# High and low position rows interleaved: four position transfers a phase in place of eight

## What is computed

```
x = x + L0(group_norm(x))     # 12 heads of 16 channels, all 1024 keys, softmax
x = x + L1(group_norm(x))     # the same heads, keys within a 7 by 7 window, and 16 register keys
```

```
rel_h = einsum('bhwc,hkc->bhwk', q, Rh)      # one value for each query and key row
rel_w = einsum('bhwc,wkc->bhwk', q, Rw)      # one value for each query and key column
scores = q @ k.T * 16**-0.5 + rel_h[..., :, None] + rel_w[..., None, :]
```

## Time and profile before

| What | Value |
|---|---|
| median of three executions | 6088.66 us (6077.25 to 6094.65) |
| the profiled execution | 6093.63 us, its span 6091.8 us |
| TensorE (PE) busy | 4712.5 us, 77% |
| VectorE (DVE), ScalarE (ACT), GpSimd (POOL) busy | 51%, 43%, 15% |
| mean granted clock of TensorE | 0.861 of full |
| DMA on SP's queue | 184672 packets, 266.11 MB, 15.5% of 16 engines' span |

### The profile page before, as it was taken

One profiled execution on the slowest core, in us unless ns is written; L12 is line 12 of the kernel. 1 busy time (PEld: TensorE's weight loads), 2 busy tenths in 40 slices (PEclk: granted clock), 3 DMA queues, 4 the chain that ended last, 5 costly groups with the idle time before them and its releaser, 6 DMA issues.

```text
span 6091.8 us, 97943 instructions
## 1 busy us (share of the span) xinstructions
PE 4712.5 (77%) x32598; PEld 2332.9 (38%) x32598; DVE 3078.8 (51%) x5558; ACT 2622.6 (43%) x3955; POOL 892.4 (15%) x1899
## 2 busy tenths in 40 slices
PE   3768877788777878777878777787778877778788
PEld 2233443444424444343433434434344443434334
DVE  2536555455554545544545454555545455545553
ACT  1333434344453444434445354444534445344454
POOL 3111100111101111011111111111011110111100
PEclk6777888888888988888889888888889889888898
DMA  5223221322213322123221223222133221332211
GB/s 102 61 59 74 49 70 55 80 64 63 56 49 80 71 62 65 39 75 76 70 62 46 72 63 77 64 58 64 50 80 69 63 65 36 80 76 70 57 35 32
DMA packets 231273, 386.23 MB, mean 63 GB/s; under 512 B 53788, under 2 KB 129120, under 8 KB 230752
## 3 DMA queue, kind: packets, MB, share of 16 engines
q1 hardware_dynamic: 184672, 266.11, 15.5%
q10 hardware_dynamic: 21504, 75.51, 6.3%
q0 software_dynamic: 24576, 37.80, 3.8%
HBM read 227.79 MB, written 88.08 MB: 52 GB/s over the span
## 4 chain that ended last, share of the span: by engine, by line
PE 40%; DMA 27%; SPq 23%; DVE 5%; issue 4%; ACT 2%; DVEq 0%; POOL 0%; ACTq 0%
DMA AR<-biases 15%; SPq L488 15%; PE P L1123 8%; PE P L1141 7%; PE P L1085 7%; DMA biases<-xn 6%; PE P L948 4%; PE P L949 4%; SPq L500 4%; DMA queries<-oraw 3%; DMA A<-mrow 3%; DVE mx L891 2%; SPq L475 2%; SPq L467 2%; PE P L1173 2%
## 5 line engine op out<-in xcount | busy, mean ns | idle before, releaser
L891 DVE TENSOR_REDUCE mx<-P 128x1 f32<-128x512 f32 x3072 | 1906.3, 682 | 1375.5 <-PE P L1085 1367.7
L761 ACT ACTIVATE probs<-P 128x1024 f32<-128x1024 f32 x1536 | 1505.4, 1022 | 1298.4 <-PE P L1141 1296.0
L1085 PE MATMUL P<-K,AR 96*128 96x256 f16 x6144 | 1163.0, 299 | 618.5 <-DMA AR<-biases 592.9
L777 ACT ACTIVATE probs<-P 128x320 f32<-128x320 f32 (+3 forms) x1632 | 638.9, 436 | 887.8 <-PE P L1194 545.5
L1085 PEld LDWEIGHTS P<-K,AR 96*128 96x128 f16 x6144 | 552.1, 104 | 1211.6 <-issue 398.9
L1141 PE MATMUL P<-AR,K 113*128 113x512 f16 x3072 | 951.2, 394 | 2.2 <-DVE mx L891 1.2
L1123 PE MATMUL P<-probs,V 128*17 128x512 f32 x6144 | 860.7, 634 | 9.9 <-ACT probs L761 9.9
L897 DVE TENSOR_REDUCE mxc<-P 128x1 f32<-128x336 f32 (+1 forms) x1536 | 646.5, 475 | 368.7 <-PE P L1094 368.4
L1061 PE MATMUL P<-QA,Z 128*128 128x64 f16 x3072 | 267.9, 253 | 302.9 <-DMA biases<-xn 225.4
L1141 PEld LDWEIGHTS P<-AR,K 113*128 113x128 f16 x3072 | 223.4, 99 | 716.8 <-ACT probs L761 528.9
L1194 PE MATMUL P<-A,K 113*128 113x320 f16 (+2 forms) x1536 | 467.5, 316 | 13.7 <-ACT probs L777 12.7
(11 more groups left out here) (120 smaller groups left out, 3740.5 us busy)
## 6 DMA issues: line engine op xcount, KB each, us to landing
AR<-biases SPq DMA_DIRECT2D x768, 128.0 KB
AR<-queries ACTq DMA_DIRECT2D x96, 512.0 KB
biases<-xn SPq DMA_DIRECT2D x192, 256.0 KB, 7.2
AR<-queries ACTq DMA_DIRECT2D x96, 256.0 KB
K<-oraw POOLq DMA_DIRECT2D x384, 64.0 KB, 4.7
xin<-in_x_dram SPq DMA_DIRECT2D x16, 768.0 KB, 9.4
queries<-oraw SPq DMA_DIRECT2D x384, 32.0 KB, 5.0
QA<-queries SPq DMA_DIRECT2D x192, 64.0 KB, 3.5
```

Of the source, the lines that this page charges most:

```text
L761: nc.scalar.activation(probs[:, u % RING, j:j + 2, :], P[:, b:b + 2, :], ACT.Exp).then_inc(p_done[0], 1)
L777: nc.scalar.activation(probs[:, full % RING, j, 0:n], P[:, step % SCORES[1], 0:n], ACT.Exp).then_inc(p_done[1], 1)
L891: V_.reduce_max(mx[:, n // 2, n % 2:n % 2 + 1], bank, AX.X).then_inc(used, 1)
L1085: last = mm(bank[:, QD * (v % 2):QD * (v % 2) + QD], AR[0:ROWS_MAX[0], part % SLOTS, v, c, j, 128 * q:128 * q + 128], K0[0:ROWS_MAX[0], h, ...
```

## The change

`biases` is laid out with the key index outermost and the high or low part behind it, so that high and low rows of one key lie side by side. The rows of `AR` and the patterns of `K0` take the same order: row 2k is the high and row 2k + 1 the low part of key k. The source of a fill is then 32 evenly spaced rows of 4 KB. A fill is four DMAs, one for each table and block of 16 keys, each of which writes the two equal variants from one source that is read twice (256 KB written a DMA). `biases_away` writes rows that are 16 KB apart. The count on `ar_in` goes from ten to six DMAs a phase.

```diff
@@ -236,7 +236,7 @@
         K0 = sb("K0", [128, NH, S], F16)
         A1, K1 = sb("A1", [128, NH, S], F16), sb("K1", [128, NH, KW], F16)
         queries = nc.dram_tensor("queries", (G, 2, D, 4, GH, QD), F16).ap()
-        biases = nc.dram_tensor("biases", (G, 2, 2, 32, 4, GH, QD), F16).ap()
+        biases = nc.dram_tensor("biases", (G, 2, 32, 2, 4, GH, QD), F16).ap()
         mid = nc.dram_tensor("mid", (B, 128, TT, C), F32).ap()
         V = [sb(f"V{n}", [128, TT, NH, D + 1]) for n in range(2)]
         vreg = sb("vreg", [128, G, 128])
@@ -333,7 +333,7 @@
         res_done = sems("res_done")
         out_in = sem("out_in")
         PER_ITEMS = [PHASES[n] * (ITEMS[n] + 1) for n in range(2)]
-        PER_Q, PER_K, PER_QA, PER_AR = 12 * 16, 12 * 16, 4 * 16, 10 * 16
+        PER_Q, PER_K, PER_QA, PER_AR = 12 * 16, 12 * 16, 4 * 16, 6 * 16
         PER_QUERIES, PER_BIASES = (8 * 16, 16 * 16), 4 * 16
         PER_MROW = (VAR * 16, 16)
         SUM_STEPS, POOL_STEPS = 3 * TT - 2, 3 * TT - 2 + 5
@@ -444,8 +444,8 @@
             def static_rows():
 
                 sp.wait_ge(rows_done, 1)
-                for r, n in ((0, 0), (16, 0), (32, 1), (48, 1)):
-                    sp.dma_start(K0[r:r + D, :, :],
+                for r, n in ((0, 0), (1, 0), (32, 1), (33, 1)):
+                    sp.dma_start(K0[r:r + 2 * D - 1:2, :, :],
                                  oneh[0:D, n:n + 1, :].broadcast_to((D, NH, S))).then_inc(rows_in, 16)
                 for r, n in ((48, 0), (80, 1)):
                     sp.dma_start(K1[r:r + 32, :, 0:S],
@@ -472,7 +472,7 @@
                 for s, (t, ready) in enumerate(((relhi, relhi_done), (rello, rello_done))):
                     sp.wait_ge(ready, (im * G + g + 1) * RELS)
                     for table in range(2):
-                        sp.dma_start(biases[g, table, s].rearrange("k a h n -> (k a) h n"),
+                        sp.dma_start(biases[g, table, :, s].rearrange("k a h n -> k a (h n)"),
                                      t[:, table, :, :]).then_inc(biases_out[g], 16)
 
             def fill_slot(im, p):
@@ -482,11 +482,13 @@
                     sp.wait_ge(st_done[0], im * STEPS[0] + (p - SLOTS + 1) * STEPS[0] // PHASES[0])
                 else:
                     sp.wait_ge(biases_out[g], (im + 1) * PER_BIASES)
-                for v in range(VAR):
-                    for table, first in enumerate((D * (v // 2), D * (v % 2))):
-                        src = biases[g, table, :, first:first + D, 2 * half:2 * half + 2, :, :]
-                        sp.dma_start(AR[32 * table:32 * table + 32, p % SLOTS, v, :, :, :],
-                                     src.rearrange("s k a h n -> s k (a h n)")).then_inc(ar_in[p], 16)
+                for table in range(2):
+                    for b in range(2):
+                        rows_ = biases[g, table, D * b:D * b + D, :, 2 * half:2 * half + 2, :, :]
+                        rows_ = rows_.rearrange("k s a h n -> (k s) (a h n)")
+                        same = slice(2 * b, 2 * b + 2) if table == 0 else slice(b, VAR, 2)
+                        sp.dma_start(AR[32 * table:32 * table + 32, p % SLOTS, same, :, :, :],
+                                     rows_.unsqueeze(1).broadcast_to((32, 2, 2 * GH * QD))).then_inc(ar_in[p], 16)
 
             def operands_out(im):
```

## The result

The changed kernel takes 5096.56 us, the median of four executions (5090.06 to 5100.7), against 6088.04 us of four of the kernel before: a ratio of 0.8372, 95% interval 0.8356 to 0.8387. The stated range (4990 to 5180) holds it; the predicted 5050 us is 47 us too low. The profiled execution took 5094.08 us with a span of 5091.3 us.

What follows compares the result with a forecast made beforehand. TensorE, busy 77%, was taken as pace-maker, its idle time the time to win. Span 6091.8 − 584 (fill waits) − 230.6 (`A<-mrow` wait) − 229 (clock) = 5048, stated as 5050 us, range 4990 to 5180.

Steps and rivals of the forecast that it cites:

- Term 1, more engines: Fills of AR use 16 DMA engines, not two, 5 us a phase; of 592.9 us of waits about 9 stay: −584.
- Term 2, SP's queue: Fills no longer hold up SP's issues, so L1190's wait for `A<-mrow` goes whole: −230.6 us.
- Term 3, the clock: TensorE's half-clock stretches behind stalls return to 2.4 GHz: 14.5 us an image, −229 in all, bounds −110 and −253.
- What was priced at nothing: The write of `biases` to rows 16 KB apart: its 12.19 us wait stays; 16 us either way if 1 us off.
- Late fills: Rival: phase 3's fill lands 3 us late, with clock +87 us, 5137; chance 0.12.
- `A<-mrow` did not wait: Rival said it still waits at L1190, as group 1's `biases` write or fill 2 comes late: +296, 5346; chance 0.05.
- the clock came back: Rival said TensorE's clock stays low or sinks elsewhere as it works denser: +229, 5280; chance 0.05.
- the DMA did spread: Rival said the split goes by the copies, so fills stay on two engines at 19.8 us: about 6090; chance 0.02.
- The repeated source: Rival said it confines each fill DMA to one engine, 39.6 us a phase: +735, at least 6820; chance 0.01.

Runs made afterwards that it cites:

- rows16_early: The kernel before with fills by DMAs of 16 rows each for phases 0, 1 and 2 alone, phases 3 to 5 filled as before: 5665.06 us, ratio 0.9294.
- Outer4: The changed kernel with eight DMAs a fill and the source rows cut into 4 groups, so outermost dimension 4: 5259.54 us, ratio 0.8642.
- rows16: The kernel before with its old layout, not interleaved, and eight DMAs of 16 rows a fill, each writing two equal variants: 5105.94 us, ratio 0.8383.
- eight_dmas: The changed kernel with eight DMAs of 32 rows a fill, one for each variant, no row read twice: 5097.0 us, ratio 0.8369.
- outer8: The changed kernel with eight DMAs a fill and the source rows cut into 8 groups, so outermost dimension 8: 5099.44 us, ratio 0.8379.

## Why the prediction was right, and where it was off

- **Term 1, more engines: right.** The share of 0.13 had been read as two engines, and the runs with 4, 8 and 16 show the row of them. The price of 5 us a fill fits 1.05 MB at 211 GB/s. Predicted −584, measured −585.1. So close a hit is partly luck, as two small misses offset each other: phase 3 did not wait at all where I had 5 us, and the start kept 7.8 us where I had 4. Phase 3 had less room than I had counted, 12.2 us from issue to need in place of 14.2, but its fill was through sooner: the DMA share falls to 0.32 in 2344 to 2346 and to 0.00 behind it, 2 us before TensorE comes. With query rows, `biases` and the fill in flight, 2338 to 2340 moved 366 GB/s, where my bounds had taken 241 as the most.
- **Term 2, SP's queue: right.** −230.6 predicted and measured, and rows16_early shows that it comes from the fills of phases 0 to 2 alone. There was more to spare than I had counted: TensorE reached L1192 23.9 us after the issue, and I had 19 (2659 to 2678). The eight fill issues took SP 3.61 us in place of 5.2.
- **Term 3, the clock: the mechanism right, the size off.** This is the term that makes the 47 us. I had −229; TensorE's busy time fell by 184.4. The same thirteen images in the kernel before and in the changed one, each stretch cut at the same instructions (the second number behind the stretch is TensorE's busy time, the third from the end its granted clock):

```profile
773.90:5593.90 4820.00, 3773.21 (x26429) 1891.05 (x26429) 2485.40 (x4485) 2130.43 (x3172) 707.36 (x1508) 0.87 0.26 64
```

```profile
666.50:4656.90 3990.40, 3610.92 (x26429) 1844.34 (x26430) 2480.25 (x4485) 2126.15 (x3172) 707.54 (x1508) 0.95 0.36 77
```

  The thirteen images gave 162.3 us, 12.5 each. What follows them, one image more, went from 410.52 to 399.42 us busy and gave 11.1: 173.4 us for 14 images where I had 14 times 14.5 = 203. The ten other stalls all lie before 773.90; there the busy time went from 528.78 to 517.76, 11.0 us where I had 26. The 14.5 us came from one image, and its low stretches were longer than most. Redone for the thirteen images that have all five stalls, TensorE's busy time at the low clock behind them is 23 to 32 us, 27 on average, against the 31.55 of my sample; my factor of 0.46 on those 27 us gives the 12.5 us measured. The stall for `A<-mrow` in a later image of the kernel before, the stretch behind it at half clock and the one after that:

```profile
5664.10:5669.70 5.60, 5.59 (x34) 2.48 (x35) 3.04 (x6) 2.75 (x6) 0.63 (x4) 0.50 0.01 3
5669.70:5673.60 3.90, 3.72 (x20) 1.91 (x18) 2.92 (x6) 1.90 (x5) 2.12 (x5) 0.99 0.00 0
```

  There the low clock lasts 5.6 us behind the wait for `A<-mrow`, in the image I took 9.5. Spread over the 77 waits that went (63 and 14), 184.4 us are 2.4 us each. The bound of −110 for half of the return is a little off, since half of 229 is 114; 184.4 lies inside the bounds either way.
- **What was priced at nothing: right.** The wait for `biases<-xn` fell from 225.4 to 219.9 us with the new rows in DRAM.
- **Rivals.** Late fills did not come: the tightest fill was there in time. Outer4 shows what they would have cost with four engines: 91.9 us of waits for fills, a part of its 163 us. `A<-mrow` did not wait, the clock came back (mean 0.933, as said near 0.93), and the DMA did spread. The repeated source (copies in the second dimension) kept 16 engines.
- **Interleaving and fewer DMAs** are two of the change's three parts, and neither carries the gain. I had not priced them apart; rows16 and eight_dmas do. What the interleaving gives over 16-row DMAs is 32 partitions a DMA, for 9 us at most.

## What to carry to other kernels

Look at the DMA share while one transfer runs alone. Here 0.13 meant two of 16 engines, and the cause was the outermost dimension of the source, not the bytes. Sixteen rows outermost in the old layout would have given the same, so first change the order of dimensions, and only then the data. A slow transfer also held the queue that issued it, and the landing of what came behind it, so look there for its second price; and take what the clock gives back from all stalls of the trace, not from one image.

## What was new about the hardware

- Into 32 partitions sixteen engines moved 211 GB/s, eight 166, four 98 and two 53. Sixteen engines on DMAs of 16 partitions each moved 130, less than eight did on 32.
- DMAs on two engines slowed their issuer, SP, to 1.7 us a DMA (16 in 27.03 us), where four fill DMAs took 1.72 us in all at 2525.72 above. With eight engines the same number of issues took 11 us, with 16 engines 7.3, in these rows of SP from outer8 and eight_dmas:

```profile
2514.67 11.07 SPq L492 DMA_DIRECT2D AR<-biases  x16
```

```profile
2509.69 7.27 SPq L489 DMA_DIRECT2D AR<-biases  x16
```
